# Attention on one NeuronCore: exponentials and triangles a step ahead, side work interleaved in quarters, norms and convolutions moved

## The chip, the cores and the metric
The kernel runs on one core of one Trainium2 chip, as one launch. The metric is device time in microseconds; lower is better. Engines: PE (TensorE), DVE (VectorE), ACT (ScalarE), POOL (GpSimd), SP (SyncE, which issues the DMAs). Each works through its own queue of instructions in order and waits at semaphores for the others.

## What is computed
Four batches of 512 tokens with 128 channels go through six residual blocks, named by their letters in the code, `ABACDC`: A is a mixture of eight experts, B eight layers of linear attention, C (twice) attention and a mixture of four experts, D a state-space scan. The change touches the attention of block C:

```python
x = x + _attn(x, ln1_w, ln1_b, conv_w, attn_w, proj_w, 16)
...
h = _layernorm(x, ln_w, ln_b)           # x comes in through a plain layernorm too
h = causal depthwise conv of width 3 over time
q, k, v = split(h @ attn_w)             # 16 heads of 8
q = q * cos + rotate_half(q) * sin      # k alike
scores = q @ k.T / sqrt(8), causal
y = softmax(scores) @ v @ proj_w
```

## The kernel before
Channels lie on partitions, time on the free axis; a batch is 128 x 512. Before the attention each batch needs a plain norm and a second one with weights, computed together: `pe_double`, `dve_centre`, `act_square`, then `act_first` and `dve_first` (L319 to L321), `act_second` and `dve_second` (L325, L327). The result, `ha`, goes through the convolution (`dve_conv` for batch 0, L1600 to L1603; `pool_conv` on POOL for batches 1 to 3, L1536 to L1545) into `res`.

Work on a batch has two parts. The *side work* makes what the attention needs, in 60 uses of two PSUM banks (5 and 6, in turn): for each 128 tokens a projection to q, k, v (L1302), whose result DVE rotates (`rope`, L1626 to L1633) and ACT and DVE split into three bf16 parts, which POOL spreads (L1558 to L1564); transposes of keys, queries, and queries with their maxima ("again", L1314), which ACT copies out (L1427, L1434) and DVE for even queries (L1651); and the maxima of scores per query, a product (L1325), a mask (L1329) and a DVE reduction (L1660) each. The *attention* of a batch has 16 steps, j = 4g + k: head group g of four heads, key tile k of 128 keys. A step has scores on PE (L1345, two pairs of heads r = 0, 1, four PSUM banks, `512 - 128k` queries), exponentials on ACT (L1479, one for each r), the triangle of the diagonal block on POOL (L1581) and values on PE (L1355). After each group ACT copies the sums (L1487), PE turns them (L1367) and DVE divides.

Steps of batch b run beside the side work of batch b + 1, which is cut into 16 steps too: `USES_BY_STEP` says how many of the 60 uses are issued by the end of each, and the `side` functions of ACT, DVE and POOL have matching cuts. Batch 0's side work stands ahead of everything, batch 3's attention runs beside no side work but beside norms of the next part (`NORM_STEPS`). The order is written out by hand. On PE a step is:

```python
if j + 1 < STEPS:
    scores(b, j + 1)
if b + 1 < NB:
    for n in range(USES_BY_STEP[j - 1] if j else 0, USES_BY_STEP[j]):
        side(b + 1, n)
values(b, j)
```

ACT does `exps(b, j)`, a copy of sums where a group has ended, then `side(b + 1, j)`. Scores of a bank wait for the exponential that empties it; exponentials wait for values two steps back, since their output `pt` has four buffers; values wait for the triangles. A side use waits until its bank is freed.

## Time and profile before
| | us |
|---|---|
| median of 3 runs (lowest, highest) | 2113.06 (2109.19, 2114.18) |
| profiled execution, its own time | 2111.17 |
| its span, from first to last instruction | 2109.4 |
| busy PE, DVE, ACT, POOL | 1770.9, 1530.9, 1334.9, 654.1 |
| first stage C from its first centring to its last value | 954 to 1276.4 |
| second stage C, the same | 1622.9 to 1948.8 |

All rows of the trace are of the profiled execution. A line such as L1479 is a line of the kernel before; "idle before" is the time for which the engine stood still ahead of an instruction, and the arrow names who ended it. PE's busy time is a union of pipelined matmuls, so two rows may overlap. PEclk is the share of TensorE's full clock that was granted: 1.0 is 2.4 GHz, 0.5 is 1.2 GHz.

### The profile page before, as it was taken

The page shows a single profiled execution, that of the slowest core. Times are in us where ns is not written, and L with a number is a line of the kernel's source. Part 1 is how long each engine was busy: PE and PEld are TensorE (multiplying, and loading weights), DVE is VectorE, ACT ScalarE, POOL GpSimd, SP SyncE. Part 2 cuts the span into 40 slices and gives each one's busy share as a digit, 9 for nine tenths or more (in the row PEclk, how much of TensorE's full clock was granted, in tenths as well). Part 3 has the DMA queues.
Part 4 walks back from the last instruction along what each step waited for, and adds up shares of the span by engine and source line. Part 5 has one row for each costly group of instructions (what it writes and reads, how often), then busy time and mean ns, then how long its engine had stood idle before and what let it go on. Part 6 is the DMA issues. An engine that isn't in the chain of part 4 may idle for free.

```text
span 2109.4 us, 24691 instructions
## 1 busy us (share of the span) xinstructions
PE 1770.9 (84%) x8806; PEld 1110.2 (53%) x8806; DVE 1530.9 (73%) x2489; ACT 1334.9 (63%) x2121; POOL 654.1 (31%) x731
## 2 busy tenths in 40 slices
PE   8999798898898889996677789995776677777998
PEld 6887466665566558883233326881222232232786
DVE  6888687778787668878666545875998855664686
ACT  6998577767777679995355565556544345556554
POOL 1444111101111014445422231221898522223131
PEclk9999899999999979998899999997899679999999
DMA  3221000000000003210000001100000000000110
GB/s 100 75 76 52 15 18 18 1 18 18 18 18 11 0 13 104 70 61 15 1 1 1 1 1 46 65 1 9 3 3 32 0 1 1 1 1 1 56 56 21
DMA packets 23770, 52.89 MB, mean 25 GB/s; under 512 B 2336, under 2 KB 6816, under 8 KB 23648
## 3 DMA queue, kind: packets, MB, share of 16 engines
q1 hardware_dynamic: 23648, 51.30, 7.7%
q8 instruction: 71, 1.16, 0.2%
q14 instruction: 51, 0.42, 0.1%
HBM read 49.66 MB, written 1.64 MB: 24 GB/s over the span
## 4 chain that ended last, share of the span: by engine, by line
PE 56%; DVE 22%; ACT 16%; issue 4%; POOL 2%; DMA 1%; POOLq 0%; ACTq 0%; DVEq 0%; SPq 0%
PE ps L553 9%; PE ps L555 9%; PE ps L554 9%; DVE arena L1940 5%; DVE arena L1660 5%; PE ps L1355 3%; PE ps L782 3%; PE ps L785 3%; PE ps L1325 3%; ACT arena L1479 2%; PE ps L783 2%; PE ps L1314 2%; ACT arena L1427 2%; PE ps L1345 2%; DVE arena L1931 1%
## 5 line engine op out<-in xcount | busy, mean ns | idle before, releaser
L664 DVE TENSOR_TENSOR hid_lo<-arena,hid_hi 128x512 fp32r<-128x512 f32 x384 | 339.3, 896 | 66.9 <-ACT arena L613 65.4
L1660 DVE TENSOR_REDUCE arena<-ps 128x1 f32<-128x512 f32 (+3 forms) x352 | 213.4, 639 | 87.3 <-PE ps L1329 84.4
L553 PE MATMUL ps<-x_hi,w_hi 128*128 128x512 f32 x512 | 209.9, 410 | 2.0 <-DVE arena L756 2.0
L1581 POOL TENSOR_SCALAR_AFFINE_SELECT arena<-arena 128x256 f32<-128x256 f32 x256 | 108.2, 430 | 314.2 <-ACT arena L1479 311.7
L554 PE MATMUL ps<-x_lo,w_hi 128*128 128x512 f32 x512 | 204.0, 398 | 0.0
L555 PE MATMUL ps<-x_hi,w_lo 128*128 128x512 f32 x512 | 204.0, 398 | 0.0
L610 ACT ACTIVATE hid_hi<-ps,wslot 128x512 fp32r<-128x512 f32 x256 | 177.3, 693 | 33.7 <-PE ps L555 6.3
L1479 ACT ACTIVATE arena<-ps 128x1024 f32<-128x1024 f32 (+3 forms) x256 | 166.2, 705 | 50.0 <-PE ps L1345 49.5
L1325 PE MATMUL ps<-arena 128*128 128x512 bf16 (+3 forms) x512 | 133.7, 327 | 69.4 <-DVE arena L1660 37.8
L613 ACT ACTIVATE arena<-ps,wslot 128x512 f32<-128x512 f32 x256 | 175.0, 684 | 0.0
L1427 ACT ACTIVATE arena<-ps 128x1024 bf16<-128x1024 bf16 x64 | 65.5, 1024 | 149.8 <-PE ps L1314 149.7
L634 POOL TENSOR_TENSOR x<-x,arena 128x512 f32<-128x512 f32 x64 | 108.5, 1699 | 145.8 <-DVE arena L625 145.8
L553 PE MATMUL ps<-hid_hi,w_hi 128*128 128x512 f32 x384 | 151.6, 395 | 2.1 <-DVE hid_lo L664 2.1
L555 PE MATMUL ps<-hid_hi,w_lo 128*128 128x512 f32 x384 | 151.7, 395 | 0.0
L554 PE MATMUL ps<-hid_lo,w_hi 128*128 128x512 f32 x384 | 150.4, 392 | 0.0
L1957 POOL TENSOR_TENSOR arena<-arena 128x512 f32<-128x512 f32 x64 | 136.1, 2166 | 44.4 <-ACT arena L1882 44.4
L735 ACT ACTIVATE arena<-ps 128x512 f32<-128x512 f32 x128 | 76.4, 597 | 97.4 <-PE ps L555 97.3
L1325 PEld LDWEIGHTS ps<-arena 128*128 128x128 bf16 x512 | 42.6, 101 | 161.6 <-DVE arena L1660 98.6
L1345 PE MATMUL ps<-arena 50*128 50x256 bf16 (+3 forms) x512 | 68.3, 321 | 60.6 <-ACT arena L1479 58.0
L756 DVE TENSOR_TENSOR arena<-arena,ps 128x512 f32<-128x512 f32 x128 | 87.4, 683 | 38.6 <-ACT arena L735 38.5
L1355 PE MATMUL ps<-arena 128*32 128x512 f32 (+3 forms) x1024 | 109.1, 501 | 7.1 <-POOL arena L1581 5.1
L553 PEld LDWEIGHTS ps<-x_hi,w_hi 128*128 128x128 f32 x512 | 98.3, 192 | 29.3 <-DVE arena L756 5.2
(309 smaller groups left out, 4190.7 us busy)
## 6 DMA issues: line engine op xcount, KB each, us to landing
arena<-gates_dram SPq DMA_DIRECT2D x96, 256.0 KB, 3.5
wslot<-pack_a SPq DMA_DIRECT2D x16, 514.5 KB, 3.8
wslot<-pack_b SPq DMA_DIRECT2D x8, 900.5 KB, 4.6
wslot<-pack_c SPq DMA_DIRECT2D x8, 768.0 KB, 4.5
res<-x_in SPq DMA_DIRECT2D x4, 256.0 KB, 5.0
out_dram<-res SPq DMA_DIRECT2D x4, 256.0 KB, 2.9
con<-consts_dram SPq DMA_DIRECT2D x1, 559.0 KB, 3.9
bc_dram<-arena SPq DMA_DIRECT2D x1, 384.0 KB, 3.2
```

Source lines behind the costliest of these rows:

```text
L553: pe.matmul(ps[:, bank, :], w1, hi, start=start, stop=False)
L554: pe.matmul(ps[:, bank, :], w1, lo, start=False, stop=False)
L555: return pe.matmul(ps[:, bank, :], w2, hi, start=False, stop=stop)
L610: act.activation(hid_hi[item % 2][:, k, :], ps[:, k, :], ACT.Gelu, bias=bias)
L613: act.activation(hid32[:, k, :], ps[:, k, :], ACT.Gelu, bias=bias).then_inc(S["hi_ok"], 1)
L664: dve.tensor_tensor(hid_lo[item % 2][:, k, :], hid32[:, k, :], hid_hi[item % 2][:, k, :].bitcast(F32), ALU.subtract).then_inc(S["hid_ok"], 1)
L1325: pe.matmul(ps[:, bank, m * keys:(m + 1) * keys], qt_s[h % 2][:, h // 2, i * P:(i + 1) * P], kt_s[b % 2][:, h // 2, 0:keys], start=(m == 0 ...
L1345: mm = pe.matmul(ps[:, 2 * r + jj, 0:n], kt_s[b % 2][r0:r0 + MROWS, hp, k * P:(k + 1) * P], q2_s[b % 2][r0:r0 + MROWS, hp, k * P:SEQ], sta ...
L1355: mm = pe.matmul(ps[32 * m:32 * m + 32, 4, k * P:SEQ], vc[b % 2][:, k, 4 * g + m, :], pt[:, (2 * j + m // 2) % NPT, m % 2, 0:SEQ - k * P], ...
L1479: act.activation(pt[:, u % NPT, :, 0:n], ps[:, 2 * r:2 * r + 2, 0:n], ACT.Exp, scale=SCALE).then_inc(S["exp_ok"], 1)
L1660: dve.tensor_reduce(neg_max[:, i, heads[0]:heads[-1] + 1:step], ps[:, bank, 0:len(heads) * keys].rearrange("p (m k) -> p m k", k=keys), AX ...
L1957: pool.tensor_tensor(ch[:, s, t, :], hst[:, s, t, :], c_s[:, u % 2, :], ALU.mult).then_inc(S["ch_ok"], 1)
```

## The change
- ACT issues the exponentials of step j + 1, and POOL the triangles of step j + 1, in loop step j; before it was those of step j. ACT's copy of sums now stands ahead of them.
- The side work runs two steps ahead (`LEAD = 2`, `ahead`): its steps 0 and 1 of batch b + 1 stand in loop steps 14 and 15 of batch b - 1, and for batch 1 ahead of the loop. The last two loop steps of batch 2 have none. The cuts of the side work and the order of its first uses are changed.
- On PE the uses of a side step are spread over four quarters: after the scores of r = 0, of r = 1, the values of r = 0, of r = 1. Values of a half wait for one triangle.
- `dve_first` and `dve_second` of batches 2 and 3, and `act_second`, move from the start to loop steps 2 to 8 of batch 0. For this ACT copies their variances out of PSUM to `sq` (two new instructions of 128 x 512).
- POOL's convolutions of batches 2 and 3 move to loop steps 6 to 10 of batches 0 and 1, one instruction a step. Batch 1's stays.
- There are three buffers of values in place of two (the third in `rstd`); POOL fills its padding in loop steps 11 and 12 of batch 0.

The diff, cut (of the scores and values the new form alone; the split of `pool_conv` into five calls and most of the new cuts of the side functions are left out):

```diff
@@ -150,6 +150,7 @@
+        vc.append(rstd[:, :, :].rearrange("p i (h d) -> p i h d", d=32))
@@ -300,6 +301,8 @@
             act.wait_ge(S["ln_log"], 4 * n + t + 1)
+            if t >= 2:
+                act.activation(sq[:, t, :], ps[:, VAR_BANKS[t], :], ACT.Copy)
             act.activation(rstd[:, t, :], rstd[:, t, :], ACT.Exp, scale=-0.5).then_inc(S["ln_rs"], 1)
@@ -316,7 +319,8 @@
             dve.wait_ge(S["ln_rs"], 4 * c["ln"] + t + 1)
-            dve_done(dve, dve.tensor_tensor(sq[:, t, :], rstd[:, t, :], ps[:, VAR_BANKS[t], :], ALU.mult))
+            var = sq[:, t, :] if t >= 2 else ps[:, VAR_BANKS[t], :]
+            dve_done(dve, dve.tensor_tensor(sq[:, t, :], rstd[:, t, :], var, ALU.mult))
             dve.tensor_tensor(sq[:, t, :], sq[:, t, :], rstd[:, t, :], ALU.mult).then_inc(S["dl_v"], 1)
@@ -1261,7 +1265,7 @@
-        SIDE_USES = ([("qkv", 0, 0), ("qkv", 1, 0), ("key", 0, 0), ("query", 0, 0), ("qkv", 2, 0)]
+        SIDE_USES = ([("qkv", 0, 0), ("qkv", 1, 0), ("qkv", 2, 0), ("key", 0, 0), ("query", 0, 0)]
@@ -1272,7 +1276,12 @@
-        USES_BY_STEP = [2, 4, 9, 13, 18, 23, 26, 29, 37, 43, 47, 49, 55, 59, 60, 60]
+        USES_BY_STEP = [2, 3, 5, 9, 13, 18, 23, 26, 29, 36, 41, 44, 48, 53, 58, 60]
+        LEAD = 2
+        def ahead(b, j):
+            return [(b + 1 + (j + LEAD) // STEPS, (j + LEAD) % STEPS)] if b + 1 + (j + LEAD) // STEPS < NB else []
@@ -1284,6 +1293,10 @@
+        ACT_NORMS = {3: 2, 7: 3}
+        DVE_NORMS = {2: (True, 2), 4: (False, 2), 6: (True, 3), 8: (False, 3)}
+        CONV_STEPS = [6, 7, 8, 9, 10]
@@ -1330,32 +1343,34 @@
+            def scores(b, j, r):
...
+                if j == 0 and r == 0:
...
+                hp = 2 * g + r
+                if 32 * b + 2 * j + r >= 2:
+                    pe.wait_ge(S["exp_ok"], 32 * q + 2 * (j - 1) + r + 1)
+                for jj in range(2):
+                    r0 = 64 * jj
+                    mm = pe.matmul(ps[:, 2 * r + jj, 0:n], kt_s[b % 2][r0:r0 + MROWS, hp, k * P:(k + 1) * P],
+                                   q2_s[b % 2][r0:r0 + MROWS, hp, k * P:SEQ], start=True, stop=True)
+                mm.then_inc(S["s2_mm"], 1)
+            def values(b, j, r):
...
+                if k == 0 and r == 0 and 4 * b + g:
...
+                pe.wait_ge(S["sel_ok"], 32 * q + 2 * j + r + 1)
+                if (b, j, r) == (2, 0, 0):
+                    pe.wait_ge(S["pad_ok"], 2 * c["attn"] + 2)
+                for m in (2 * r, 2 * r + 1):
+                    mm = pe.matmul(ps[32 * m:32 * m + 32, 4, k * P:SEQ], vc[b % 3][:, k, 4 * g + m, :],
...
+                if r:
+                    mm.then_inc(S["pv_mm"], 1)
@@ -1372,21 +1387,39 @@
-            pe.wait_ge(S["pad_ok"], c["attn"] + 1)
-            for n in range(USES):
-                side(0, n)
-            pe.wait_ge(S["ln_out"], 4 * c["ln"] + NB)
-            scores(0, 0)
+            pe.wait_ge(S["pad_ok"], 2 * c["attn"] + 1)
+            def side_step(b, j):
+                for n in range(USES_BY_STEP[j - 1] if j else 0, USES_BY_STEP[j]):
+                    side(b, n)
+            for j in range(STEPS):
+                side_step(0, j)
+            side_step(1, 0)
+            pe.wait_ge(S["ln_xc"], 4 * c["ln"] + NB)
+            pe.wait_ge(S["ln_rs"], 4 * c["ln"] + NB)
+            pe.wait_ge(S["dl_v"], 4 * c["attn"] + 2)
+            for r in range(2):
+                scores(0, 0, r)
+            for j in range(1, LEAD):
+                side_step(1, j)
...
-                    if j + 1 < STEPS:
-                        scores(b, j + 1)
-                    if b + 1 < NB:
-                        for n in range(USES_BY_STEP[j - 1] if j else 0, USES_BY_STEP[j]):
-                            side(b + 1, n)
-                        if j + 1 == STEPS:
-                            scores(b + 1, 0)
-                    values(b, j)
+                    def sides(quarter):
+                        for to, at in ahead(b, j):
+                            first = USES_BY_STEP[at - 1] if at else 0
+                            many = USES_BY_STEP[at] - first
+                            for n in range(many * quarter // 4, many * (quarter + 1) // 4):
+                                side(to, first + n)
+                    for r in range(2):
+                        if j + 1 < STEPS:
+                            scores(b, j + 1, r)
+                        elif b + 1 < NB:
+                            scores(b + 1, 0, r)
+                        sides(r)
+                    for r in range(2):
+                        values(b, j, r)
+                        sides(2 + r)
@@ -1501,21 +1533,32 @@
-                if j < NB - 1:
-                    act_second(act, c, j + 1)
+                if j == 0:
+                    act_second(act, c, 1)
+                elif j == 1:
+                    act_first(act, c, 3)
+            side(1, 0)
+            exps(0, 0)
+            for j in range(1, LEAD):
+                side(1, j)
...
-                    exps(b, j)
...
+                    if j + 1 < STEPS:
+                        exps(b, j + 1)
+                    elif b + 1 < NB:
+                        exps(b + 1, 0)
...
-                    if b + 1 < NB:
-                        side(b + 1, j)
-                    else:
+                    if b == 0 and j in ACT_NORMS:
+                        act_second(act, c, ACT_NORMS[j])
+                    for at in ahead(b, j):
+                        side(*at)
+                    if b == LATE:
...
@@ -1571,20 +1614,35 @@
-            pool_conv(pool, c, range(1, NB))
+            for step in range(5):
+                pool_conv(pool, c, 1, step)
+            for j in range(LEAD):
+                side(1, j)
+            def triangles(step):
+                for u in (2 * step, 2 * step + 1):
...
+                    pool.wait_ge(S["exp_ok"], 32 * q0 + u + 1)
...
+            triangles(0)
...
-                    for r in range(2):
-                        u = 32 * b + 2 * j + r
...
-                        pool.wait_ge(S["exp_ok"], 32 * q0 + u + 1)
...
-                    if b + 1 < NB:
-                        side(b + 1, j)
+                    if STEPS * b + j + 1 < STEPS * NB:
+                        triangles(STEPS * b + j + 1)
+                    for at in ahead(b, j):
+                        side(*at)
+                    if b < 2 and j in CONV_STEPS:
+                        pool_conv(pool, c, b + 2, CONV_STEPS.index(j))
+                    if (b, j) == (0, 11):
+                        pool.wait_ge(S["ln_out"], 4 * c["ln"] + NB)
+                        pool.memset(vc[2][:, :, :, DH:DH + 1], 1.0)
+                    if (b, j) == (0, 12):
+                        pool.memset(vc[2][:, :, :, DH + 1:32], 0.0).then_inc(S["pad_ok"], 1)
...
-            for v in vc:
+            for v in vc[0:2]:
@@ -1621,12 +1679,14 @@
-                if i == 0 and q >= 2:
-                    dve.wait_ge(S["pv_mm"], 16 * (q - 1))
+                if i == 0 and b == 3:
+                    dve.wait_ge(S["pv_mm"], 16 * (q - 2))
+                if i >= 2:
+                    dve.wait_ge(S["split_ok"], 4 * q + i - 1)
...
-                dve.tensor_copy(vc[b % 2][:, i, :, 0:DH], ps[:, bank, 2 * P:3 * P].rearrange("p (h d) -> p h d", d=DH))\
+                dve.tensor_copy(vc[b % 3][:, i, :, 0:DH], ps[:, bank, 2 * P:3 * P].rearrange("p (h d) -> p h d", d=DH))\
...
@@ -1747,10 +1808,10 @@
-                if j < 2:
-                    dve_first(dve, c, j + 2)
-                elif j < 4:
-                    dve_second(dve, c, j)
+                if j == 1:
+                    dve_second(dve, c, 1)
+            for j in range(LEAD):
+                side(1, j)
@@ -1759,9 +1820,12 @@
-                    if b + 1 < NB:
-                        side(b + 1, j)
-                    else:
+                    if b == 0 and j in DVE_NORMS:
+                        first, t = DVE_NORMS[j]
+                        (dve_first if first else dve_second)(dve, c, t)
+                    for at in ahead(b, j):
+                        side(*at)
+                    if b == LATE:
```

PE's queue in loop step 3 of batch 0, before: the scores of step 4 (L1345), side step 3 with the transposes of keys and queries, a projection and the transposes with maxima (L1314, 8 for each use, and L1302), and the values of step 3 (L1355).

```order
L1345 MATMUL ps<-arena 128x512 x4
L1314 MATMUL ps<-ident,arena 128x128 x16
L1302 MATMUL ps<-par,res 128x384
L1314 MATMUL ps<-ident,arena 128x128 x8
L1355 MATMUL ps<-arena 32x128 x4
```

All uses of the step stand in one block between scores and values.

The same side uses in the new order stand in loop step 2, with the scores of step 3 (now L1357), the values of step 2 (L1369), transposes L1327 and projection L1315.

```order
L1357 MATMUL ps<-arena 128x128 x2
L1327 MATMUL ps<-ident,arena 128x128 x8
L1357 MATMUL ps<-arena 128x128 x2
L1327 MATMUL ps<-ident,arena 128x128 x8
L1369 MATMUL ps<-arena 32x256 x2
L1315 MATMUL ps<-par,res 128x384
L1369 MATMUL ps<-arena 32x256 x2
L1327 MATMUL ps<-ident,arena 128x128 x8
```

One use now follows each half of scores or values.

ACT's queue at the start of batch 1's attention, before: exponentials of steps 0, 1 and 2 (L1479; 1024, 2x384 and 2x256 wide), the copy of batch 0's last sums (L1487), part copies for the side work of batch 2 (L1417), the first keys (L1427) and odd queries (L1434).

```order
L1479 ACTIVATE arena<-ps 128x1024 x2
L1487 ACTIVATE arena<-ps 128x512
L1417 ACTIVATE arena<-arena 128x32x8 x2
L1479 ACTIVATE arena<-ps 128x2x384 x2
L1417 ACTIVATE arena<-arena 128x32x8 x2
L1427 ACTIVATE arena<-ps 128x8x128
L1434 ACTIVATE arena<-ps 48x8x128
L1479 ACTIVATE arena<-ps 128x2x256 x2
```

Part copies stand on both sides of the exponentials of step 1, and the key copy ahead of those of step 2.

The same place in the new order, from loop step 14 of batch 0 on: exponentials L1511, sums L1519, part copies L1450, keys L1460, odd queries L1467.

```order
L1511 ACTIVATE arena<-ps 128x2x128 x2
L1450 ACTIVATE arena<-arena 128x32x8 x2
L1511 ACTIVATE arena<-ps 128x1024 x2
L1450 ACTIVATE arena<-arena 128x32x8 x2
L1519 ACTIVATE arena<-ps 128x512
L1511 ACTIVATE arena<-ps 128x2x384 x2
L1460 ACTIVATE arena<-ps 128x8x128
L1467 ACTIVATE arena<-ps 48x8x128
L1450 ACTIVATE arena<-arena 128x32x8
L1511 ACTIVATE arena<-ps 128x2x256 x2
```

Both pairs of part copies moved up, the first ahead of the exponentials of step 0 and the second behind them.

## Rows read from the trace of the kernel before

**Rows 1.** The page of the whole span: busy time by engine; one of its costliest groups.
```profile
PE 1770.9 (84%) x8806; PEld 1110.2 (53%) x8806; DVE 1530.9 (73%) x2489; ACT 1334.9 (63%) x2121; POOL 654.1 (31%) x731
...
L1479 ACT ACTIVATE arena<-ps 128x1024 f32<-128x1024 f32 (+3 forms) x256 | 166.2, 705 | 50.0 <-PE ps L1345 49.5
```

**Rows 2.** Busy time by stretch; columns are named in the first row.
```profile
core 0: us, PE busy (x) PEld busy (x) DVE busy (x) ACT busy (x) POOL busy (x), PEclk, DMA share, GB/s
954.00:1024.20 70.20, 43.01 (x233) 19.07 (x231) 58.84 (x117) 27.82 (x40) 40.29 (x47) 0.85 0.04 12
1024.20:1095.20 71.00, 52.15 (x418) 21.67 (x416) 41.79 (x94) 37.44 (x56) 19.03 (x52) 0.91 0.00 1
1095.20:1166.60 71.40, 53.19 (x430) 22.52 (x426) 43.04 (x97) 37.74 (x58) 19.03 (x52) 0.93 0.00 1
1166.60:1236.90 70.30, 51.85 (x430) 22.30 (x426) 42.94 (x97) 37.76 (x58) 19.04 (x52) 0.95 0.00 1
1236.90:1276.40 39.50, 31.83 (x222) 9.80 (x222) 13.87 (x27) 28.54 (x49) 15.63 (x32) 0.87 0.00 1
...
1694.10:1767.90 73.80, 55.74 (x418) 22.32 (x416) 42.01 (x94) 37.53 (x56) 19.03 (x52) 0.85 0.00 1
```

**Rows 3.** Waits in batch 1 of the first stage C: total us, times, longest.
```profile
ACT arena L1427 <- PE ps L1314: 17.3, 8, 4.4
...
PE ps L1345 <- ACT arena L1479: 7.9, 10, 2.5
...
PE ps L1325 <- DVE arena L1660: 4.9, 14, 0.5
```

**Rows 4.** Timeline at the start of batch 1, ACT and then PE.
```profile
1094.51 1.94 ACT L1479 ACTIVATE arena<-ps 128x1024 f32<-128x1024 f32 x2 [0.30 <-PE ps L1345]
...
1099.23 0.42 ACT L1417 ACTIVATE arena<-arena 128x256 bf16<-128x256 f32 x1 [2.29 <-DVE arena L1633]
1100.65 0.42 ACT L1417 ACTIVATE arena<-arena 128x256 bf16<-128x256 f32 x1 [1.00 <-DVE arena L1633]
...
1101.82 0.35 PE L1345 MATMUL ps<-arena 50*128 50x256 bf16 x2 [2.50 <-ACT arena L1479]
...
1103.71 1.87 PE L1314 MATMUL ps<-ident,arena 128*128 128x128 bf16 x16 [0.80 <-POOL arena L1564]
```

**Rows 5.** Groups by shape in batch 1: count, busy us, mean ns, idle before.
```profile
L1660 DVE TENSOR_REDUCE arena<-ps 128x1 f32<-128x512 f32 x16 | 10.3, 687 | 3.3 <-PE ps L1329 3.2
L1479 ACT ACTIVATE arena<-ps 128x1024 f32<-128x1024 f32 x9 | 8.8, 1022 | 2.3 <-PE ps L1345 2.3
L1427 ACT ACTIVATE arena<-ps 128x1024 bf16<-128x1024 bf16 x8 | 8.2, 1024 | 17.3 <-PE ps L1314 17.3
...
L1479 ACT ACTIVATE arena<-ps 128x768 f32<-128x768 f32 x8 | 6.1, 822 | 0.0
```

**Rows 6.** Timeline of DVE in step 12 of batch 1's attention.
```profile
1155.29 3.75 DVE L1660 TENSOR_REDUCE arena<-ps 128x1 f32<-128x512 f32 x6 [0.91 <-PE ps L1329]
```

**Rows 7.** Start of stage C, DVE by shape; two lines of code, ns min/median/max.
```profile
L1660 DVE TENSOR_REDUCE arena<-ps 128x1 f32<-128x512 f32 x16 | 10.1, 686 | 1.0 <-PE ps L1329 1.0
...
L325 DVE SCALAR_TENSOR_TENSOR ha<-hb,par,sq 128x512 f32<-128x512 f32 x4 | 3.0, 745 | 0.1
L321 DVE TENSOR_TENSOR hb<-xc,rstd 128x512 f32<-128x512 f32 x4 | 2.8, 708 | 0.0
L320 DVE TENSOR_TENSOR sq<-sq,rstd 128x512 f32<-128x512 f32 x4 | 2.8, 692 | 0.1
...
L319 DVE TENSOR_TENSOR sq<-rstd,ps 128x512 f32<-128x512 f32 x4 | 2.7, 678 | 0.0
...
L327 DVE TENSOR_SCALAR ha<-ha,par 128x512 f32<-128x512 f32 x4 | 2.4, 604 | 0.1
...
L1538 POOL TENSOR_SCALAR xc<-ha,par x6: 1565/1566/1612, 996.1 to 1677.9; 128x512 f32<-128x512 f32 x6
...
L1600 DVE TENSOR_SCALAR res<-ha,par x2: 486/884/1282, 963.9 to 1631.5; 128x512 f32<-128x512 f32 x2
```

114 lines of the change are left out of this document (49 added, 65 removed).

## The prediction

> **What bounds the kernel now.** I read the page first. TensorE is busy for 84% of the span [rows 1], but the change touches only stage C, so the page's shares decide nothing and the stage is cut into stretches. [rows 2] has them: the start of the first stage C (70.2 us, to the first exponential), its batches 0, 1 and 2 (71.0, 71.4, 70.3), in which the attention of one batch and the side work of the next run together, and batch 3 alone (39.5). The second stage C repeats them: its batch 0 takes 73.8 (shown), and by their first and last matmul its other four stretches take 71.2, 71.2, 70.2 and 39.5. The reader should see that in batch 1 no engine fills its 71.4 us: PE 53.2, DVE 43.0, ACT 37.7, POOL 19.0. The bound is a chain of hand-overs; about 18 us of PE's time per batch is idle.
>
> The waits of batch 1 name the hand-overs [rows 3]: PE stands 7.9 us before scores until ACT's exponentials have emptied the banks, and 4.9 us until a DVE maximum has freed one of the two side banks; ACT itself waits 17.3 us for transposes. Why the exponentials are late is in the timeline [rows 4]: after the values of step 0, PE waits 2.50 us, until 1101.82, for the exponentials of step 1. These stood in ACT's queue behind two copies of rotated queries and keys, which came at 1099.23 and 1100.65 because DVE had only then made them. What follows is 16 transposes that take 1.87 us; the granted clock has dropped to 1.2 GHz after that idle stretch. Over batch 1 the granted clock is 0.93 [rows 2], so about (1 - 0.93) x 2 x 71.4 = 10 us run at the lower level.
>
> **The change, part by part.** The program's own time of the profiled execution is 2111.17 us (span 2109.4 and 1.8 around it); the sum is made against it.
>
> *Exponentials and triangles one step ahead, side work two steps ahead.* No instruction is added. ACT now does exponentials j+1 before the side work, so PE's scores never meet an exponential that waits behind a copy: the 7.9 us should go whole. In exchange the copies that free side banks come behind a pair of exponentials.
>
> *Quarters.* PE's side operations are spread between two halves of scores and two of values. In the old order maxima stand in PE's queue in rows of up to six, and PE waits before most (14 times in batch 1 [rows 3]), for DVE needs 0.69 us for one [rows 5] (about 0.62 from start to start: six took 3.75 us [rows 6]) and PE less. Spread out, half of the 4.9 us should lie beside values: 2.5. The half-rate stretch behind the 2.50 us gap costs PE about half of its length where PE is what is waited for; I take 5 us of the 10, and that half of them goes: 2.5. So batch 1 goes to 71.4 - 7.9 - 2.5 - 2.5 = 58.5 us.
>
> Checked from below, by the busiest engine of each loop step in the new order. Durations from [rows 5], less the 0.1 us by which ACT's rows overlap (two exponentials of 1.02 stand in 1.94 us [rows 4]) and 0.08 on DVE. Step 0, ACT: copy of sums 0.6, two exponentials of 0.82, key copy 1.02, odd queries the same, part copy 0.42 [rows 4], less 0.6: 4.1. Step 11, DVE: 5 maxima, 3.0. Likewise for all: 4.1, 3.9, 3.3, 3.4, 4.6, 2.7, 2.2, 3.7, 2.6, 2.5, 2.4, 3.0, 3.0, 2.5, 4.1, 2.5, together 50.5 us. (PE is the busiest in steps 1, 5, 9 and 13 alone.) The same sum for the old order gives about 48, and it takes 71.4: it loses 23 us in hand-overs. At 58.5 the new one loses 8. Following the four queues through the new steps 14, 15 and 0 to 5, with each semaphore of the code, the tightest place is the first key transposes, which wait for DVE, ACT and POOL in turn, and the lengths stay near the sum. I choose 58.5, with 51 and 66 as ends (66: only half of the two waits goes and no clock, 71.4 - 6).
>
> *Norms of batches 2 and 3 moved into batch 0.* They take ten DVE instructions from the start: per batch 0.68 + 0.69 + 0.71 + 0.75 + 0.60 = 3.43 us [rows 7], so 6.9 us from a stretch of 70.2 in which DVE is busy 58.8. Their cover was partly waiting: at the first queries and keys DVE would have waited for ACT and POOL anyway. I give back about 5 us. Against it, the first exponential now stands behind the rotated parts 0 and 1 of batch 1: behind the last copy come one projection (about 0.6), a rotation and a part copy (from one part copy to the next it is 1.42 [rows 4], and the last lasts 0.42), 2.4 us. Net -2.5 us for the start. The two new ACT copies of variances, some 0.6 us each in a stretch where ACT is busy for 27.8 of 70.2, lie under ACT's idle time; without that cover they would cost 1.2 us.
>
> In batch 0 the ten come back, with four ACT instructions: in loop step 2 DVE has 2.5 + 1.9 = 4.4 where ACT's 3.3 was the most (+1.1), step 4 stays under ACT's 4.6, step 6 gets +1.9 and step 8 +1.3 on DVE, and step 7 +1.2 on ACT: 5.5 us. There is no earlier batch to finish there (-1.2), and the first pair of exponentials stands bare (+1.9). Batch 0: 58.5 + 5.5 - 1.2 + 1.9 = 64.7.
>
> *Side work ends two steps earlier.* Batch 2's last two loop steps hold attention alone: 4.1 + 2.5 become 0.8 + 1.9, so 58.5 - 3.9 = 54.6.
>
> *Convolutions of batches 2 and 3 on POOL in steps 6 to 10.* One instruction of 1.57 us at most [rows 7] per step beside triangles of 0.8, in steps of 2.2 to 3.7 us, with a step to spare: nothing. If a POOL instruction made a triangle late, values would wait for what is beyond the step, under 1 us each.
>
> *The third value buffer* takes a wait from the rotations; the two memsets (1.6 us, POOL, batch 0) have the same cover. *Batch 3* keeps its order on ACT; halves of values may start one triangle earlier: -1, from 0 to -3.
>
> Per stage C: start -2.5; batch 0 71.0 to 64.7, -6.3; batch 1 -12.9; batch 2 70.3 to 54.6, -15.7; batch 3 -1: together -38.4. Twice is -76.8; the second batch 0 was 2.8 us longer at a clock of 0.85 [rows 2], and I let half of that go, -1.4. 2111.2 - 78.2 = 2033.0. The three runs' median is 1.9 above the profiled execution, so **2035 us**.
>
> **A rule against the change.** The first stage C has one instruction that meets a busy POOL: the multiplication of batch 0's convolution takes 1.28 us there and 0.49 in the second stage, where no POOL memset runs beside it [rows 7]. Against that, 15 POOL instructions of the convolutions ran beside DVE's maxima (which read PSUM) in the old start, and those took 0.69 [rows 7] as in batch 1 [rows 5]. So a price can be had from rows: in batch 0, five norm instructions on DVE now share steps 6 and 8 with POOL's convolutions, and each may wait for one whole POOL instruction, 5 x 1.57 = 7.9 us per stage.
>
> The Trainium skill, page "SBUF — State Buffer", section "SBUF: two separate sides", says that DVE and GpSimd take a shared pair of ports as an exclusive lock for a whole instruction, when DVE has two SBUF inputs or a two-port mode. By that rule the price would be met in full and the sum would be 2051; by the row of 1.28 us a small part of it is. The sum above goes by the rows, with nothing.
>
> **The rivals.**
> *(a) The bank hand-over stays.* Two side banks and DVE's 43 us are unchanged, and a maximum between two halves of values makes values wait instead. Then the exponentials' wait goes (7.9) and little else, batch 1 at 63.5. Three batches 5 us longer, twice: 2065. For it: PE's waits for DVE are many and short [rows 3], and a step with five maxima needs 3 us of DVE whatever PE does. Against: DVE is idle 28 us of a batch.
> *(b) Slower: the copies are late.* Each of the 12 copies of transposes per batch now stands behind a pair of exponentials, on average 2 x 0.705 = 1.4 us [rows 1]. If the next side operation waits for each, 12 x 1.4 = 17 us are added where 12.9 are won, +4 per batch, and 2135 in all. It decides from the point where more than nine of the twelve are waited for. Against it: most transposes' banks are wanted again only two operations later, and the tables give the heavy ones steps with short exponentials.
> *(c) Close to the busiest engine.* Batches at 51: 7.5 us x 6 less, 1990. For it: the hand-over sum of 50.5. Against: no stage of this kernel reaches such a sum now.
> *(d) The lock*, 2051, as priced.
> *(e) It doesn't do it.* Another in-order wait, for instance the key transposes on POOL's spreads behind the triangles, takes the place of the removed one: 2111.
>
> **How the numbers follow.** The forecast (2010 to 2052) 0.50; (a) 0.26; (b) 0.05; (c) 0.10; (d) 0.05; (e) 0.04. The likeliest case gives the time. The range runs from 2000, inside (c), to 2085, beyond (a) and (d) for batches at 66: it leaves out (b), (e) and part of (c) and (a), about 0.2. A measurement can tell 0.3%, 6 us, from no change. Faster: the forecast, (a), (c), (d) and a little of (e), 0.92; same 0.03; slower, (b) and a rest, 0.05.
>
> **What would show it.** Right: stretches of about 65, 58 and 55 us between the last values of batches 0, 1 and 2; PE's wait for exponentials under 2 us in batch 1; its granted clock at 0.96 or more; the first exponential of the first stage C at about 1021.7; POOL's triangles never waited for. Wrong in size: PE's waits for the maxima staying near 5 us, or long waits of PE for key copies (rival b). A norm instruction of 1.3 us or more in steps 6 and 8 of batch 0 would show (d). The prediction is wrong if batch 1 takes over 66 us, or if the start grows, because the two side steps ahead of the first exponentials cost more than the norms give.

## The result

The changed kernel takes 2082.18 us (median of 4, 2077.99 to 2084.22) against 2113.62 for the kernel before on the same chip (2109.19 to 2117.28): ratio 0.985, interval 0.9825 to 0.9874. It is faster, by 31 us where 78 were forecast (2035 us, range 2000 to 2085). Its profiled execution took 2084.22 us (span 2082.5).

The page of the whole span and its group of exponentials, which answer to [rows 1]:
```profile
PE 1816.3 (87%) x8806; PEld 1116.9 (54%) x8806; DVE 1541.3 (74%) x2489; ACT 1337.5 (64%) x2125; POOL 660.8 (32%) x735
...
L1511 ACT ACTIVATE arena<-ps 128x1024 f32<-128x1024 f32 (+3 forms) x256 | 168.1, 703 | 132.6 <-PE ps L1357 132.1
```
TensorE runs as many instructions as before and is busy 45 us longer, in a span 27 us shorter. ACT used to wait 50 us for scores and now waits 132: the exponentials stand early in their queue, as intended. The new 45 us are the surprise.

Busy time by stretch, which answers to [rows 2] (same columns): the start and batches 0 to 3 of the first stage C.
```profile
954.00:1026.40 72.40, 51.21 (x235) 21.35 (x234) 56.06 (x116) 26.87 (x41) 24.23 (x39) 0.69 0.03 11
1026.40:1095.00 68.60, 57.79 (x416) 21.49 (x415) 49.07 (x103) 38.95 (x59) 29.72 (x57) 0.95 0.01 1
1095.00:1161.50 66.50, 60.11 (x427) 23.43 (x427) 44.65 (x98) 37.95 (x57) 26.31 (x58) 0.92 0.00 1
1161.50:1225.70 64.20, 57.60 (x426) 22.58 (x422) 41.61 (x90) 38.22 (x57) 19.22 (x52) 0.95 0.00 1
1225.70:1264.50 38.80, 31.99 (x224) 10.68 (x222) 13.83 (x27) 28.68 (x49) 14.74 (x32) 0.91 0.00 1
```
The reader should see that PE now fills 60.1 of batch 1's 66.5 us, where it filled 53.2 of 71.4. TensorE stands idle for 6.4 us of the batch, where it was idle for 18.2: it is now the bound, at 90%.

The waits of batch 1, which answer to [rows 3] (total us, times, longest):
```profile
ACT arena L1511 <- PE ps L1357: 19.3, 13, 4.2
...
ACT arena L1460 <- PE ps L1327: 4.8, 4, 1.8
...
PEld ps L1338 <- DVE arena L1720: 6.2, 15, 0.8
...
PE ps L1357 <- ACT arena L1511: 1.8, 2, 1.2
PEld ps L1369 <- POOL arena L1626: 1.7, 6, 0.5
...
PE ps L1338 <- DVE arena L1720: 0.2, 1, 0.2
```
PE's wait for exponentials went from 7.9 to 1.8 us, its wait for maxima from 4.9 to 0.2, ACT's for transposes from 17.3 to 4.8. The waits that the change aimed at are nearly gone (weight loads, PEld, still wait 6.2 us for maxima beside PE's work, 10.8 before), and the batch is only 4.9 us shorter. What took their place is in PE's timeline (start us, us, what, how many records): step 4 of batch 1, with the two halves of its values.
```profile
1119.48 0.34 PE L1357 MATMUL ps<-arena 50*128 50x384 bf16 x2
1119.75 0.39 PE L1338 MATMUL ps<-arena 128*128 128x256 bf16 x2
1119.98 0.27 PE L1342 MATMUL ps<-mask_qk,ident 128*128 128x256 bf16 x1
1120.18 1.05 PE L1369 MATMUL ps<-arena 128*32 128x512 f32 x4
1121.17 0.39 PE L1338 MATMUL ps<-arena 128*128 128x256 bf16 x2
1121.40 0.27 PE L1342 MATMUL ps<-mask_qk,ident 128*128 128x256 bf16 x1
1121.60 1.05 PE L1369 MATMUL ps<-arena 128*32 128x512 f32 x4
```
A value matmul has 32 columns of weights and writes 32 partitions of the bank; each leaves two records. A half (two matmuls) takes 1.05 us. The same step in a kernel that leaves all four in one piece (the first experiment):
```profile
1113.10 1.06 PE L1370 MATMUL ps<-arena 128*32 128x512 f32 x8
```
Four last as long as two. They run at the same time, and side operations between the halves part them, so that the time is paid twice; the experiments below show that it is these operations. The busy time of the value line alone in batch 1 says what it comes to (PE, then PEld), in the kernel before and in the changed one:
```profile
1095.20:1166.60 71.40, 13.47 (x132) 2.61 (x128) 0.93 0.00 1
```
```profile
1095.00:1161.50 66.50, 22.04 (x128) 4.17 (x128) 0.92 0.00 1
```
That is +8.6 us of PE in a batch that took 8.0 us more than forecast. The two need not be the same microseconds: without the halves the batch is 6.3 us shorter (66.6 to 60.3, below).

### The profile page after: what moved, and what is told of

Same layout as the page of the kernel before. It is cut to its first block, busy times and chain, and to the rows that moved or that the text cites. A ratio compares the mean times of both kernels' runs of the same rounds, so it can differ in the third digit from the quotient of the medians.

```text
span 2082.5 us, 24722 instructions
## 1 busy us (share of the span) xinstructions
PE 1816.3 (87%) x8806; PEld 1116.9 (54%) x8806; DVE 1541.3 (74%) x2489; ACT 1337.5 (64%) x2125; POOL 660.8 (32%) x735
## 4 chain that ended last, share of the span: by engine, by line
PE 60%; DVE 20%; ACT 15%; issue 3%; POOL 1%; DMA 1%; POOLq 0%; DVEq 0%; ACTq 0%; SPq 0%
PE ps L557 9%; PE ps L559 9%; PE ps L558 9%; PE ps L1369 5%; DVE arena L2004 5%; PE ps L1338 4%; DVE arena L1720 3%; PE ps L786 3%; PE ps L789 3%; PE ps L787 2%; PE ps L1327 2%; ACT arena L1511 2%; PE ps L1357 2%; ACT arena L1460 2%; DVE arena L1995 1%
## 5 line engine op out<-in xcount | busy, mean ns | idle before, releaser
L1720 DVE TENSOR_REDUCE arena<-ps 128x1 f32<-128x512 f32 (+3 forms) x352 | 218.8, 641 | 86.3 <-PE ps L1342 81.4
L1511 ACT ACTIVATE arena<-ps 128x1024 f32<-128x1024 f32 (+3 forms) x256 | 168.1, 703 | 132.6 <-PE ps L1357 132.1
L1338 PE MATMUL ps<-arena 128*128 128x512 bf16 (+3 forms) x512 | 140.1, 333 | 42.4 <-DVE arena L1720 12.6
L1369 PE MATMUL ps<-arena 128*32 128x512 f32 (+3 forms) x768 | 118.7, 485 | 9.2 <-ACT arena L1519 7.0
L1460 ACT ACTIVATE arena<-ps 128x1024 bf16<-128x1024 bf16 x64 | 65.6, 1025 | 89.0 <-PE ps L1327 88.9
L760 DVE TENSOR_TENSOR arena<-arena,ps 128x512 f32<-128x512 f32 x128 | 87.5, 683 | 38.6 <-ACT arena L739 38.5
L638 POOL TENSOR_TENSOR hb<-hb,arena 128x512 f32<-128x512 f32 x32 | 42.1, 1317 | 225.5 <-DVE arena L632 225.5
```

The costliest lines, as they stand in the source:

```text
L638: pool.tensor_tensor(dst[:, t, :], dst[:, t, :], gated[:, item % 2, :], ALU.add).then_inc(S["added"], 1)
L1338: pe.matmul(ps[:, bank, m * keys:(m + 1) * keys], qt_s[h % 2][:, h // 2, i * P:(i + 1) * P], kt_s[b % 2][:, h // 2, 0:keys], start=(m == 0 ...
L1369: mm = pe.matmul(ps[32 * m:32 * m + 32, 4, k * P:SEQ], vc[b % 3][:, k, 4 * g + m, :], pt[:, (2 * j + m // 2) % NPT, m % 2, 0:SEQ - k * P], ...
L1511: act.activation(pt[:, u % NPT, :, 0:n], ps[:, 2 * r:2 * r + 2, 0:n], ACT.Exp, scale=SCALE).then_inc(S["exp_ok"], 1)
L1720: dve.tensor_reduce(neg_max[:, i, heads[0]:heads[-1] + 1:step], ps[:, bank, 0:len(heads) * keys].rearrange("p (m k) -> p m k", k=keys), AX ...
```

## The experiments

They ran in three groups of four, each group on one chip beside the kernel before, in three rounds; the kernel before took 2115.9 (e1 to e4), 2115.5 (e5 to e8) and 2118.4 us (e9 to e12) there, as medians. The changed kernel's own ratio stands against 2113.6. Differences within a group are the safer ones; across groups the ratios and the medians can say a few us more or less. This table has each one's ratio with its interval, and the stretches of both stages C in us: from the first centring to the first exponential, and on to the last value matmul of batches 0, 1, 2 and 3.

```
kernel                 us      ratio, interval         first stage C             second stage C
before                 2115.9  1                       68.7 71.0 71.4 70.3 39.5  71.2 73.8 71.2 70.3 39.5
after                  2082.2  0.985  0.9825-0.9874    72.6 68.6 66.6 64.2 38.8  69.1 68.7 66.6 64.2 38.8
e1_whole_values        2047.8  0.967  0.9647-0.9693    68.4 65.2 60.3 60.0 37.8  71.1 65.3 57.8 56.6 37.3
e2_block               2076.0  0.9817 0.978-0.9853     70.8 71.2 65.1 62.9 38.3  71.6 69.0 65.0 62.9 38.3
e3_halves_alone        2135.7  1.0092 1.0068-1.0117    72.7 75.8 76.2 73.5 39.6  69.9 76.9 76.2 72.8 37.3
e4_norms_back          2074.2  0.9794 0.9774-0.9815    76.4 63.1 66.3 63.0 37.1  75.3 62.6 64.2 61.7 38.4
e5_whole_norms_back    2052.6  0.9696 0.9676-0.9717    73.7 61.6 59.0 56.6 37.3  74.8 59.9 59.1 59.9 37.8
e6_convs_back          2047.4  0.9673 0.9649-0.9697    76.2 59.6 61.5 60.3 38.0  75.3 59.7 59.0 56.6 37.3
e7_not_ahead           2102.1  0.9929 0.9909-0.9949    76.5 70.7 68.9 63.3 40.7  75.5 70.1 68.2 63.2 40.1
e8_exps_first          2057.4  0.9716 0.9692-0.9739    74.2 61.7 61.4 60.2 43.1  73.5 61.7 61.4 60.2 43.1
e9_sides_between       2088.2  0.9841 0.9806-0.9877    70.7 68.7 66.6 64.2 39.3  71.3 71.2 64.5 63.1 39.3
e10_two_waits          2051.5  0.9676 0.9655-0.9698    69.3 66.1 59.2 60.0 37.5  71.2 63.2 59.3 60.0 37.5
e11_triangles_late     2068.6  0.9757 0.9735-0.9779    71.8 73.2 62.0 56.2 39.4  71.6 71.4 60.8 57.5 38.1
e12_lead_one           2089.7  0.9862 0.983-0.9894     72.6 73.2 65.0 64.6 39.7  70.7 70.5 65.0 64.6 39.7
```

### Are the halves the cost?

**e1_whole_values**, the changed kernel with a step's four value matmuls together:
```
-                pe.wait_ge(S["sel_ok"], 32 * q + 2 * j + r + 1)
+                if r == 0:
+                    pe.wait_ge(S["sel_ok"], 32 * q + 2 * j + 2)
...
                     for r in range(2):
                         values(b, j, r)
+                    for r in range(2):
                         sides(2 + r)
```


> The changed kernel, with the two halves of values in one piece again (one wait for both triangles, quarters 3 and 4 of the side uses behind them). Theory T1, column groups: four value matmuls side by side take as long as two, so halves with something between them cost PE twice; in batch 1 of the changed kernel PE's value rows hold 22.0 us against 13.5 before. Undone, they should be back at about 13.5 us and each of the three overlapped batches should lose 5 to 8.5 us: 2082 - 6 x 7 = 2040, from 2031 to 2052. Theory T2, side banks: the spreading itself covers the wait for maxima, and with less of it the batches stay at 64 to 68 us: 2075 to 2090.

34 us less than the changed kernel by the medians (38 by the ratios), inside the range of the first theory. In batch 1 PE is busy 50.8 us instead of 60.1, of it 13.05 on values instead of 22.04. First the busy time of batch 1, then that of the value line alone:
```profile
1090.20:1150.40 60.20, 50.77 (x425) 21.61 (x427) 43.71 (x98) 37.87 (x57) 26.27 (x58) 0.94 0.01 1
```
```profile
1090.20:1150.40 60.20, 13.05 (x128) 2.57 (x128) 0.94 0.01 1
```

**e3_halves_alone**, the kernel before with only its values in halves and half of the side uses between them:
```
-            def values(b, j):
+            def values(b, j, r):
-                for m in range(4):
+                for m in (2 * r, 2 * r + 1):
...
+                    values(b, j, 0)
+                    if b + 1 < NB:
+                        for n in range(middle, last):
+                            side(b + 1, n)
+                    values(b, j, 1)
```


> The kernel before with one edit: values in two halves, and the second half of the step's side uses between them. T1 says PE's value rows grow from 13.5 towards 22 us in each overlapped batch and the program gets slower by 3 to 8 us a batch: 2113 + 6 x 5 = 2143, from 2125 to 2160. T2 says the waits for maxima shrink and it is faster than before: 2085 to 2105.

The same edit costs here too, 0.9%, with batches 0 to 2 longer by 2.5 to 5 us. The value line alone in its batch 1:
```profile
1099.30:1175.50 76.20, 25.20 (x132) 4.57 (x128) 0.93 0.01 1
```
The values take 11.7 us more than before and PE in all 9.7 (62.9 against 53.2), but the batch only 4.8: the other half lies in time in which this kernel's PE stood idle anyway (18.2 us before, 13.3 now).

**e9_sides_between** and **e10_two_waits** tell which part of the edit does it, the side matmuls between or the second wait. The former has e1's single wait and the changed kernel's order, the latter the changed kernel's two waits and e1's order.

> The changed kernel, but a step's value matmuls wait once, for both triangles, ahead of the first half; the side matmuls stay between the halves. Theory (what parts the four column groups is the other matmuls between the halves, not the second wait): each half still lasts as long as a whole did, batch 1 stays at 66 to 67 us and the time within 6 us of the changed kernel, 2076 to 2088. Rival (it is the second wait, since back-to-back halves were seen to run together only where none stood between): about 2050.

> The changed kernel with its two waits, but no side matmuls between the halves (quarters 3 and 4 stand behind both). Theory: the second triangle is mostly done when the first half is issued, so the four groups run together again in most steps and the time is 2048 to 2058 us, close to the one with the whole values. Rival (the second wait parts them even where it is already met): 2075 to 2085.

Both came out as the theory says, 2088.2 (at the upper end of its range) and 2051.5: 37 us apart on one chip, by the place of the side matmuls alone. The value line alone in batch 1, of e9_sides_between and then of e10_two_waits:
```profile
1095.10:1161.70 66.60, 22.09 (x132) 4.18 (x128) 0.92 0.00 1
```
```profile
1089.50:1148.70 59.20, 12.80 (x128) 2.56 (x128) 0.97 0.00 1
```
The second wait does not part the four (weight loads of values waited for a triangle once in this batch of e10_two_waits, 0.3 us); side matmuls between them do. Whether their shape matters was not tried.

### What are the parts of the change worth?

**e2_block**, e1 with each step's side uses in one block behind the scores:
```
                             scores(b + 1, 0, r)
-                        sides(r)
+                    for r in range(4):
+                        sides(r)
                     for r in range(2):
                         values(b, j, r)
-                    for r in range(2):
-                        sides(2 + r)
```


> The changed kernel with no interleaving: scores, then all side uses of the step, then values in one piece, as before, but exponentials and side work still ahead. T1 says values are back at 13.5 us, but the waits for maxima (4.9 us per batch before) return: 2 to 4 us per batch over the kernel with whole values, so 2050 to 2065. T2 says that interleaving carried the gain: 2090 or more.

**e7_not_ahead**, e5 (below) with exponentials and triangles in their own step:
```
             for b in range(NB):
                 for j in range(STEPS):
+                    exps(b, j)
...
-                    if j + 1 < STEPS:
-                        exps(b, j + 1)
-                    elif b + 1 < NB:
-                        exps(b + 1, 0)
...
-                        triangles(STEPS * b + j + 1)
+                        triangles(STEPS * b + j)
```


> As e5_whole_norms_back, but exponentials stand ahead of the side work of their own step and triangles in their own step, as in the kernel before, instead of one step ahead. Theory: exponentials ahead took away waits of the tensor engine of some 6 us in each of batches 0 to 2 (7.9 us before, 1.8 after in batch 1), so about 30 us slower, some 2070. Rival: interleaving alone gives the exponentials their time, and the order on ScalarE and GpSimd is worth under 8 us: about 2045.

**e11_triangles_late**, e1 with the last of these edits alone (exponentials stay ahead).

> As e1_whole_values, but the triangles stand in their own step on GpSimd, behind the spreads of the step before, and the exponentials stay a step ahead. Theory: of the 50 us that exponentials and triangles one step later cost, the exponentials hold nearly all, since scores wait for them; triangles alone cost up to 10 us, 2048 to 2058. Rival: values wait for triangles behind a spread that waits for its part, in some 6 steps of a batch by 1 us or more: 2065 or above.

**e12_lead_one**, e1 with `LEAD = 1`.

> As e1_whole_values, but the side work runs one step ahead of the attention loop instead of two. Theory: a lead only shifts which side uses fall into which step, the loop of batch 3 gets none either way, and the start has one use less of batch 1: within 10 us of 2048. Rival: the lead is what lets batch b+1's first scores not wait for the last transposes and copies (steps 15 and 0), and without its second step 3 us are lost at each of three joins and two stages: 2065 or above.

The order ahead is the largest part: without it 50 us are lost (2102.1 against 2052.6, one group), more than either expectation had. In its batch 1 PE waits for exponentials again:
```profile
PE ps L1357 <- ACT arena L1513: 10.0, 9, 2.4
```
Triangles alone cost 21 us on e1 (17 against e10_two_waits of the same group), twice what I had allowed. 14 of these lie in the two batches 0: POOL's spreads wait for a part from ACT, the triangle stands behind them, and values wait. Batches 1 have convolutions on POOL too and lose only 1.7 and 3.0 us, so the convolutions alone do not explain it. Batch 0 of the first stage in e11_triangles_late:
```profile
POOL arena L1603 <- ACT arena L1452: 17.3, 5, 7.5
...
PE ps L1370 <- POOL arena L1628: 5.8, 3, 3.4
```
Interleaving is worth 28 us (2076.0 against 2047.8, one group), between the two ranges that I had given: with the side uses in one block PE waits for maxima again, 1.7 us in batch 1 of e1 and, in that of e2_block:
```profile
PE ps L1338 <- DVE arena L1721: 4.2, 13, 0.5
```
The second step of lead is worth 42 us (2089.7; 38 against e10_two_waits of the same group). My prediction gave the lead only 3.9 us, in batch 2. The rival put on record had it right that the lead matters; but it is not lost at the joins alone: batch 1 takes 65.0 us at lead one, and of its steps 15 is 2.7 us, 9 is 2.2 and 4 is 1.1 longer than in e1, while 8 and 1 are 2.0 and 1.3 shorter. Lead one also shifts which uses share a step with which exponentials, and this was not separated from it.

### The start and the norms

**e4_norms_back**, the changed kernel with the second norms of batches 2 and 3 in the start again, and **e5_whole_norms_back**, the same on e1:
```
-        ACT_NORMS = {3: 2, 7: 3}
-        DVE_NORMS = {2: (True, 2), 4: (False, 2), 6: (True, 3), 8: (False, 3)}
+        ACT_NORMS = {}
+        DVE_NORMS = {}
...
             for j in range(STEPS):
                 side(0, j)
-                if j == 1:
-                    dve_second(dve, c, 1)
+                if j < 2:
+                    if j == 1:
+                        dve_second(dve, c, 1)
+                    dve_first(dve, c, j + 2)
+                elif j < 4:
+                    dve_second(dve, c, j)
```


> The changed kernel with the second norms of batches 2 and 3 back in the start, all else as changed. My prediction had the move worth 5 us at the start and costing 5.5 us in batch 0, so no change within 3 us: 2080 to 2086 with the start about 5 us longer and batch 0 about 5 us shorter. If the start is bound by PE at the lower clock and not by DVE, putting them back costs the start 0 to 2 us and gives batch 0 5 us: 2072 to 2078.

> The changed kernel with values of a step in one piece and the second norms of batches 2 and 3 back in the start of the stage. Theory: the two are separate costs (one on the tensor engine in batches 0 to 2, one on the vector engine in batch 0), so the gains add: 2047.8 - 8.0 = about 2040 us, batch 0 about 60 us, start about 72. Rival: the norms' 8 us were free only because the tensor engine was slowed by the halves; with whole values the vector engine's start is on the path in full and the time stays at 2046 to 2050.

ACT's halves of the norms go back likewise. On the changed kernel this saves 8 us by the medians (12 by the ratios), on e1 it saves nothing (2052.6 against 2047.8, intervals that overlap): the first theory for e5 fell, the 8 us do not add. e4's time fell into the range of its second theory, but not by its mechanism. In both pairs the start is 3.7 to 6.2 us longer with the norms in it and batch 0 is 3.6 to 6.1 shorter, so the move itself comes to about nothing. The rest of e4's 8 us is in batches 1 to 3, where the code is the changed kernel's: 3.2 and 5.3 us in the two stages, with the granted clock at its lower level for 17 and 10 us of them instead of 24 and 24. What makes the clock differ there is open.

**e6_convs_back**, e5 with all 15 convolution instructions in the start, and **e8_exps_first**, e5 with the first exponentials ahead of batch 1's first parts:
```
-            for step in range(5):
-                pool_conv(pool, c, 1, step)
+            for b in range(1, NB):
+                for step in range(5):
+                    pool_conv(pool, c, b, step)
...
-                    if b < 2 and j in CONV_STEPS:
-                        pool_conv(pool, c, b + 2, CONV_STEPS.index(j))
```
```
-            side(1, 0)
             exps(0, 0)
-            for j in range(1, LEAD):
+            for j in range(LEAD):
                 side(1, j)
```


> As e5_whole_norms_back, and the convolutions of batches 2 and 3 back in the start of the stage too, on GpSimd in one piece behind batch 1's, ahead of the spreads of batch 1. Theory A (convolutions in the loop cost nothing, and in the start they hold up the first spreads of batch 1 by 10 instructions, some 14 us, of which the queue ahead takes part): 3 to 8 us slower than e5_whole_norms_back. Rival B (convolutions in the loop hold the triangles and so the values up by what they last, and in the start they are hidden): 3 to 8 us faster.

> As e5_whole_norms_back, but the first exponentials of a stage stand ahead of the first two parts of batch 1 on ScalarE. Theory: the parts wait for two rotations on the vector engine (the 3 us by which the first exponentials came late), so the start of each stage is 2 to 3 us shorter and the time 3 to 6 us less than e5_whole_norms_back. Rival: the parts come later by the two exponentials and batch 0 takes it back: within 1.5 us.

The convolutions are worth nothing measurable at either place (the intervals of e5 and e6 overlap), so neither theory's 3 to 8 us is there. Exponentials first gains nothing either, and neither of its expectations held: 2057.4, with starts of 74.2 and 73.5 us against 73.7 and 74.8. Its batches 3, whose code is e5's, took 43.1 us instead of 37.3 and 37.8, at a lower clock (0.76 in the row): 11 of the 14.6 us between the two profiled spans. The profiled execution of e8 was its slowest (2065.9); the medians are 4.7 us apart, and whether any of that is the edit's own is open. The first of the two:
```profile
1211.20:1254.30 43.10, 36.14 (x226) 10.70 (x222) 13.84 (x27) 28.69 (x49) 14.74 (x32) 0.76 0.00 1
```

## Why the prediction was wrong in size

**The step that failed** is "Quarters": I let the spreading of side operations between two halves of values win 2.5 us and cost TensorE nothing. It costs 8.6 us of PE in batch 1. The trace of the kernel before could have warned me. In it a step's four value matmuls over 512 columns take 1.06 us together (8 records, at 1098.25), while one f32 matmul over 512 columns with full weights takes as long: 1.08 us (2 records, at 1123.49 in the changed kernel), and 1.2 in the first row below. The second row is its group of values of 256 columns in batch 1, the third its transposes, and the last the values in the changed kernel (records, busy us, mean ns of one):
```profile
L1372 PE MATMUL ps<-arena,par 128*128 128x512 f32 x2 | 1.2, 666 | 0.0
...
L1355 PE MATMUL ps<-arena 128*32 128x256 f32 x32 | 2.6, 391 | 0.0
...
L1314 PE MATMUL ps<-ident,arena 128*128 128x128 bf16 x96 | 7.8, 235 | 1.2 <-POOL arena L1564 0.8 <-issue 0.2
```
```profile
L1369 PE MATMUL ps<-arena 128*32 128x256 f32 x32 | 4.4, 391 | 0.0
```
32 records of 0.391 us are 12.5 us, yet PE was busy for 2.6 with them: they lay over each other, nearly five deep (each matmul leaves two records); in the changed kernel it is nearly three. The overlap alone proves nothing: 96 transposes of 0.235 us stand in 7.8 us, nearly three deep, and these are issued one behind the other with full weights. The sign is that four values cost what one full matmul costs. Undone, the cut gives 34 of the 47 us by which I missed. Of the other 13, by e1's stretches against the forecast's, 7.4 lie in the two batches 2 and 4.6 in the two starts. It also brought the size that I had named as proof against me, a batch 1 over 66 us; the other sign, a longer start, came in the first stage alone. The check from below (50.5) used whole values for PE, so it could not see it; with halves PE's own 60.1 us is the larger sum.

The Trainium skill, page "TensorE: Matmul & The Clock Gate", section "Part 3: Packing small matmuls — row/col tiling", says that tiles of the array run together and that a set lasts about as long as one of its matmuls, plus some 4 ns for each further tile. By that rule a set cut in two costs twice, and the trace agrees (1.06 us for four, 1.05 for two).

**Exponentials ahead: right.** 7.9 us became 1.8. **Maxima: right in direction, small in size:** 4.9 became 0.2 where I let half go; with the values whole it is 1.7, and 4.2 without the interleaving.

**The half-rate clock: wrong.** I let half of 10 us go; batch 1's granted clock is 0.92 in the changed kernel, 0.93 before, not 0.96. In e1 it is 0.94 in the first stage and 1.00 in the second.

**Batches against the forecast, once the halves are undone.** Forecast 64.7, 58.5, 54.6 and 38.5; e1 has 65.2, 60.3, 60.0, 37.8 and 65.3, 57.8, 56.6, 37.3 in its two stages. Batches 0, 1 and 3 stand. Batch 2 is 2.0 us long where the clock was full and 5.4 where it was not.

**The norms: the two terms were right, their net value is nothing.** Moved out, they give the start 3.7 to 6.2 us (forecast 5) and cost batch 0 3.6 to 6.1 (forecast 5.5).

**The start: wrong.** Forecast 2.5 us shorter; it is 3.9 longer in the first stage and 2.1 shorter in the second. The first exponential came at 1026.4 and not at 1021.7. ACT's timeline there:
```profile
1021.76 1.02 ACT L1460 ACTIVATE arena<-ps 128x1024 bf16<-128x1024 bf16 x1 [11.56 <-PE ps L1327]
1024.66 0.42 ACT L1450 ACTIVATE arena<-arena 128x256 bf16<-128x256 f32 x1 [1.87 <-DVE arena L1693]
1026.08 0.42 ACT L1450 ACTIVATE arena<-arena 128x256 bf16<-128x256 f32 x1 [1.00 <-DVE arena L1693]
1026.40 1.92 ACT L1511 ACTIVATE arena<-ps 128x1024 f32<-128x1024 f32 x2
```
From the last copy to the exponentials it is 4.6 us; before it was 1.8 (1022.39 to 1024.20 in its trace): +2.8, where I had put +2.4. That term was right, yet taking the parts away did not bring it back (e8). The clock is lower too: 0.69 in this start, 0.85 before [rows 2]. And one norm instruction of DVE takes 2.57 us, from 961.43, where it takes 0.49 later in the same start; the rows are below, at the lock. In the kernel before it was a multiplication of 1.28. DVE, the busiest engine of the start, waits longer for PE's masks (two groups of maxima in the start; their idle time was 1.0 and 2.1 us before):
```profile
L1720 DVE TENSOR_REDUCE arena<-ps 128x1 f32<-128x512 f32 x16 | 10.7, 690 | 2.0 <-PE ps L1342 1.4
L1720 DVE TENSOR_REDUCE arena<-ps 128x1 f32<-128x384 f32 x16 | 8.4, 555 | 3.8 <-PE ps L1342 3.8
```
In e1, whose code is the same in both stages, the start takes 68.4 us at a granted clock of 0.83 and 71.1 at 0.70:
```profile
956.50:1024.90 68.40, 46.11 (x235) 19.74 (x234) 54.54 (x117) 26.79 (x40) 25.05 (x39) 0.83 0.03 12
```
```profile
1598.40:1669.50 71.10, 50.70 (x235) 20.62 (x235) 54.02 (x116) 26.78 (x40) 22.41 (x36) 0.70 0.00 1
```
Why the clock stays down longer in this start than in the one before was not settled. e5 keeps starts of 73.7 and 74.8 us where the kernel before has 68.7 and 71.2, although its norms stand where they stood; some 2.8 us are the two parts, and what else of the new order does it is open.

**The convolutions and the lock.** "Nothing" was right for the convolutions (e6). The sign of rival (d), a norm instruction of 1.3 us or more in batch 0, is not there. DVE's norm instructions in batch 0, by shape:
```profile
L329 DVE SCALAR_TENSOR_TENSOR ha<-hb,par,sq 128x512 f32<-128x512 f32 x2 | 1.6, 812 | 0.0
L325 DVE TENSOR_TENSOR hb<-xc,rstd 128x512 f32<-128x512 f32 x2 | 1.6, 782 | 0.0
L324 DVE TENSOR_TENSOR sq<-sq,rstd 128x512 f32<-128x512 f32 x2 | 1.5, 774 | 0.1
L323 DVE TENSOR_TENSOR sq<-rstd,sq 128x512 f32<-128x512 f32 x2 | 1.4, 682 | 0.0
```
On average they are at most 0.08 us longer than in [rows 7]. But only one of them meets a convolution at all, and waiting of this kind is in the trace, with a part of it on the other engine. In order: all triangles of POOL (ns min/median/max) and two that ran beside norm instructions; the norm instruction that meets a convolution, and that convolution; a later convolution instruction and a small subtraction of DVE; a norm instruction in the first start, beside four memsets of POOL.
```profile
L1626 POOL TENSOR_SCALAR_AFFINE_SELECT arena<-arena x256: 399/406/920, 1029.9 to 1918.9; 128x256 f32<-128x256 f32 x128
...
1058.47 1.66 POOL L1626 TENSOR_SCALAR_AFFINE_SELECT arena<-arena 128x256 f32<-128x256 f32 x2 [1.99 <-ACT arena L1511]
...
1059.79 0.88 DVE L325 TENSOR_TENSOR hb<-xc,rstd 128x512 f32<-128x512 f32 x1
1060.12 1.99 POOL L1578 TENSOR_SCALAR res<-ha,par 128x512 f32<-128x512 f32 x1
...
1075.00 1.26 POOL L1588 TENSOR_TENSOR res<-res,xc 128x511 f32<-128x511 f32 x1
1075.13 1.22 DVE L1732 TENSOR_TENSOR arena<-arena 128x16 bf16<-128x16 f32 x1
...
961.43 2.57 DVE L331 TENSOR_SCALAR ha<-ha,par 128x512 f32<-128x512 f32 x1
```
The two triangles take 0.85 us each in place of 0.41. At 1059.79 DVE had started first, and it is POOL's convolution that takes 1.99 us in place of 1.57. At 1075.00 POOL had started first, and DVE's subtraction ends when POOL is done, after 1.22 us; four of its kind in the start of the stage take 0.23 each. By the rule of the Trainium skill, page "SBUF — State Buffer", section "SBUF: two separate sides", whichever of the two starts first keeps the shared pair of ports for its whole instruction and the other is blocked, and the trace agrees in these places (the addition of 2.57 us waited for more than one memset). So (d) had the mechanism and not the price: it let five norm instructions per stage wait for 1.57 us each, 7.9 us. What is found is 1.9 us of POOL (four triangles and the convolution) and 1.0 of DVE in batch 0, 1.0 of DVE in batch 1, and 2.1 of DVE in the first start. What these cost in time was not measured by itself. "A rule against the change" said that one instruction alone met a busy POOL in the old trace; that was incomplete: the same small subtraction took 0.65 us there beside L1538, and L327 0.90 beside a memset in the second stage.

**The other rivals.** (a) gave 2065 by a hand-over that stays; the hand-over went, and the time lay beyond. (b), late copies: PE waited 2.7 us in batch 1 for copies of keys and odd queries, and 3.2 before. (e), no gain, did not happen. (c), 1990, is not reached by any kernel here.

The fastest versions are e1 and e6, at 2047.8 and 2047.4 us and not to be told apart: 3.3% below the kernel before and 1.7% below the changed one.

## What to carry to other kernels

Before something is put between the matmuls of a set, ask whether they run at the same time: if four small ones last as long as one full one (1.06 us here), they are one instruction for the planner, and side matmuls between them cost a whole one more. Price an edit on every engine that it touches, above all on the one that becomes the bound once the waits are gone. In-order queues want each engine's critical work ahead of its side work, by one step for exponentials and triangles (50 us here), and side work early by two steps and not one (42 us).

## What the runs showed of the hardware

A set of value matmuls (128x32 weights, 512 columns of data) takes 1.06 us for four and 1.05 for two; the four run together also when a second wait stands between the second and third (value line 12.80 us in batch 1), and not when side matmuls do (22.09).

DVE and POOL hold each other up in some pairs of instructions: a DVE subtraction of 128x16 took 1.22 us beside a POOL addition of 1.26 and 0.23 otherwise, a DVE addition of 128x512 2.57 beside memsets and 0.49 otherwise, a POOL multiplication 1.99 beside a DVE product and 1.57 otherwise, a POOL triangle 0.85 beside norm instructions and 0.41 otherwise. DVE's maxima, which read PSUM, ran beside POOL's convolutions in 0.69 us.

The granted clock falls in one pass through the same instructions and not in another. Batches 1 and 2 of e1, second stage, after 60.2 and 60.0 us at 0.94 and 0.91 in the first:
```profile
1734.80:1792.60 57.80, 48.23 (x428) 20.96 (x427) 43.70 (x98) 37.76 (x57) 26.29 (x58) 1.00 0.01 1
1792.60:1849.20 56.60, 46.65 (x421) 20.38 (x422) 41.46 (x89) 38.06 (x57) 19.07 (x52) 1.00 0.00 1
```
By the rows, the lower level (1.2 GHz) held for (1 - 0.94) x 2 x 60.2 = 7 us and likewise 11 us, and cost 2.4 and 3.4 us: about a third of its length. Two passes through the same two batches can so differ by some 6 us without any change in the code, which is as much as the norms were argued about.
